# Two attentions of a decoder-like block joined into one pipeline of four phases, with the weights split a phase ahead

## The reference

```python
ln_out = ln(x)
q  = ln(fp8_linear(ln_out, wq,  ...))   # 16 heads, normalised per head
k  = ln(fp8_linear(ln_out, wk,  ...))   # 8 heads
v  =    fp8_linear(ln_out, wv,  ...)
core = gqa(q, k, v)                     # softmax(q k / sqrt(128)) v, per sequence
qx = ln(fp8_linear(ln_out, wqx, ...))
kx, vx = split(ctx @ w_kv_x.T);  kx = ln(kx)
xout = gqa(qx, kx, vx)
cat  = concat(core, xout)               # 32 heads of 128
x   += fp8_round(cat / smooth) @ wproj.T * (proj_in * proj_w)
```

## Time and profile before

| | us |
|---|---|
| runs (3): median, lowest, highest | 1149.35, 1148.18, 1149.48 |
| profiled execution | 1150.45 |
| its span in the profile | 1148.5 |
| TensorE busy in it | 890.5 (78%) |
| VectorE busy | 932.7 (81%) |
| ScalarE busy | 715.9 (62%) |
| GpSimd busy | 393.4 (34%) |

### The profile page before, as it was taken

The page is one execution under the profiler, slowest core; times in us unless marked ns, Lnnn a source line. Parts: engine busy times, 40 slices in busy tenths (PEclk is TensorE's granted clock), DMA queues, the critical chain, the costliest instruction groups (busy, mean ns, idle before and its releaser), DMA issues. The chain is left out here.

```text
span 1148.5 us, 23844 instructions
## 1 busy us (share of the span) xinstructions
PE 890.5 (78%) x6878; PEld 787.9 (69%) x6878; DVE 932.7 (81%) x2442; ACT 715.9 (62%) x2471; POOL 393.4 (34%) x498
## 2 busy tenths in 40 slices
PE   3720056621899999999999369999999999997738
PEld 3710033321788888888898358999999999996627
DVE  7989989878889889989988448888888888886460
ACT  3445034363888888888888457777777777774303
POOL 0008910000344444444444433333343333323024
PEclk9865589855999999999999679999999999998559
DMA  6021200001100000000000220000000000000400
GB/s 223 1 100 50 70 0 1 0 0 67 45 2 1 0 0 0 0 0 0 0 0 1 60 69 6 11 6 5 5 9 5 5 5 5 0 0 1 152 19 19
DMA packets 18266, 26.96 MB, mean 23 GB/s; under 512 B 1264, under 2 KB 15408, under 8 KB 17456
## 3 DMA queue, kind: packets, MB, share of 16 engines
q1 hardware_dynamic: 17840, 25.41, 6.5%
q0 software_dynamic: 384, 1.05, 0.3%
HBM read 23.83 MB, written 2.62 MB: 23 GB/s over the span
## 5 line engine op out<-in xcount | busy, mean ns | idle before, releaser
L1214 POOL TENSOR_TENSOR c_pn<-c_p,c_rsum 128x256 f32<-128x256 f32 x64 | 39.6, 619 | 216.4 <-DVE c_rsum L1337 216.4
L1251 DVE TENSOR_REDUCE c_v<-c_sq 128x6 f32<-128x768 f32 x64 | 60.7, 949 | 54.4 <-ACT c_sq L1394 54.2
L1214 POOL TENSOR_TENSOR s_pn<-s_p,s_rsum 128x256 f32<-128x256 f32 x64 | 39.6, 618 | 141.0 <-DVE s_rsum L1337 141.0
L1228 POOL TENSOR_TENSOR s_cat<-s_tb,s_mb 128x512 fp32r<-128x512 bf16 x64 | 73.9, 1154 | 34.6 <-DVE s_tb L1292 34.6
L1251 DVE TENSOR_REDUCE s_v<-s_sq 128x6 f32<-128x768 f32 x64 | 60.7, 949 | 28.5 <-ACT s_sq L1394 28.1
L1228 POOL TENSOR_TENSOR c_cat<-c_tb,c_mb 128x512 fp32r<-128x512 bf16 x64 | 74.0, 1156 | 28.8 <-DVE c_tb L1292 28.8
L1453 PE MATMUL s_pj_ps<-wp,s_cat 128*128 128x256 f32 x512 | 78.9, 298 | 1.6 <-POOL s_cat L1228 1.6
L1453 PE MATMUL c_pj_ps<-wp,c_cat 128*128 128x256 f32 x512 | 78.1, 296 | 1.8 <-POOL c_cat L1228 1.8
L1377 ACT ACTIVATE s_p<-s_kT_sc_ps,s_nmax 128x64 f32<-128x64 f32 x256 | 76.6, 311 | 2.8 <-DVE s_nmax L1258 2.4
L1377 ACT ACTIVATE c_p<-c_kT_sc_ps,c_nmax 128x64 f32<-128x64 f32 x256 | 76.6, 311 | 2.7 <-DVE c_nmax L1258 1.8
L1417 PE MATMUL c_qo_ps<-wq,c_xqf 128*128 128x512 f32 x256 | 75.9, 419 | 0.0
(11 more groups left out here) (359 smaller groups left out, 2912.8 us busy)
## 6 DMA issues: line engine op xcount, KB each, us to landing
x_res<-in_x SPq DMA_DIRECT2D x4, 512.0 KB, 6.0
vT<-in_ctxT SPq DMA_DIRECT2D x2, 1024.0 KB, 10.5
tf_work<-in_wqT SPq DMA_DIRECT2D x2, 1024.0 KB, 6.2
tf_work<-in_wprojT SPq DMA_DIRECT2D x2, 1024.0 KB, 5.5
w_work<-in_wqxT SPq DMA_DIRECT2D x2, 1024.0 KB, 6.6
w_work<-in_wkvxT SPq DMA_DIRECT2D x2, 1024.0 KB, 8.1
c_ctx<-in_ctxT SPq DMA_DIRECT2D x16, 128.0 KB, 2.2
w_work<-in_wprojT SPq DMA_DIRECT2D x2, 1024.0 KB, 7.9
```

The source lines that it names most:

```text
L1214: nc.gpsimd.tensor_tensor(pn[:].rearrange("p (a t) -> p a t", a=4), pe_s[:].rearrange("p (a t) -> p a t", a=4), rsum[:].unsqueeze(2).broad ...
L1228: nc.gpsimd.tensor_tensor(cat[out8.o % 2][:], tb[:], mb[:], ALU.subtract).then_inc(cat_ready, 1)
L1251: norm(nc.vector.tensor_reduce(v6[:], sq[:].rearrange("p (h d) -> p h d", d=D), AX.X, ALU.add))
```

## The change

- The two attentions are one stage and one pipeline of 128 units, with no loops: all steps are written out. It has four phases of 32 units. A phase takes half the heads of one kind over all 16 tiles: phases 0 and 1 are self, 2 and 3 cross. A unit is the same as before; a tile has two units in a phase.
- Weights are held in two sets of half the size. Phase i uses set i % 2. The weights of phase 0 are prepared in the ternary stage, as before, but they are half as many. Those of phase i + 1 are prepared in phase i, for all i below 3: heads (scale, sum, mean off) in steps 1 to 24, uppers of 128x256 on ScalarE in steps 5 to 28, lowers of 128x256 on GpSimd in steps 6 to 29 (those of v in phase 0, which need a scale, on VectorE).
- On GpSimd a step's order is: pn, head, lower part, cat, conversion.
- On TensorE the query transposes stand ahead of the value product.
- On VectorE the rounding instructions are interleaved with the Newton step, and the addition to x stands ahead of the normalised key; it adds two tiles at once (128x512), after each fourth unit. The projection now sums two units in PSUM.
- SyncE loads the q weights of phase 1 in the quant stage, the rest at the start of the attention, and those of later phases when GpSimd is done with the buffers.

The core of the diff:

```diff
+def first_weights_act(act, nc, aw, raw):
     act.wait_ge(aw["scales_ready"], 4)
+    for part, kind, n in (("q", 0, QC // D), ("k", 1, KVC // D)):
+        act.wait_ge(aw["arrived"][part], 16)
...
+def first_weights_pool(pool, nc, aw, raw, col):
...
+    pool.wait_ge(aw["scales_ready"], 4)
+    for h in range(KC):
+        half = raw["v"][:, h, :]
+        nc.gpsimd.tensor_scalar(half, half, scale_col(aw, 2, h), None, ALU.mult).then_inc(aw["sums_ready"], 1)
+    pool.wait_ge(aw["sums_ready"], KC)
+    split("v", 1)
+    pool.wait_ge(aw["arrived"]["p"], 16)
+    split("p", 2)
...
+        pool.wait_ge(aw["scaled"], nth + 1)
...
+        split(part, 3 + nth)
...
+FIRST_HEAD_AT, FIRST_UPPER_AT, FIRST_LOWER_AT = 1, 5, 6
...
+        def head_item(u):
+
+            i = u.o - FIRST_HEAD_AT
+            return Head(aw, raw_w, u.phase + 1, i) if u.phase + 1 < N_PHASES and 0 <= i < N_HEADS else None
...
             def _(pool):
...
+                convert(0)
+                for s in range(UNITS + 4):
+                    u, soft, out8 = At(s), At(s - 3), At(s - 4)
                     if soft.live:
...
                             rsum[:].unsqueeze(2).broadcast_to([P, 4, S]), ALU.mult).then_inc(pn_ready, 1)
+                    head = head_item(u) if u.live else None
+                    if head:
+                        pool.wait_ge(aw["head_scaled"], head.count)
+                        nc.gpsimd.tensor_tensor(head.sum, head.sum, minus_mean[:], ALU.mult).then_inc(aw["head_sum"], 1)
+                        pool.wait_ge(aw["head_sum"], head.count)
+                        nc.gpsimd.tensor_tensor(head.w, head.w, head.sum.broadcast_to([P, D]), ALU.add
+                                                ).then_inc(aw["head_centred"], 1)
+                    w, count = piece(u, FIRST_LOWER_AT) if u.live else (None, None)
+                    if w and w.scale is None:
+                        pool.wait_ge(aw["piece_upper"], count)
+                        pool.wait_ge(aw["piece_lower"], count - 1)
+                        nc.gpsimd.tensor_tensor(w.lower, w.raw, w.upper.bitcast(F32), ALU.subtract
+                                                ).then_inc(aw["piece_lower"], 1)
                     if out8.live:
+                        pool.wait_ge(cadd_ready, out8.count())
                         wait_unit(pool, pj_done, out8.before(2))
+                        nc.gpsimd.tensor_tensor(cat[out8.n % 2][:], tb[:], mb[:], ALU.subtract).then_inc(cat_ready, 1)
...
+                    if u.live and u.half == 0 and u.turn + 1 < N_PHASES * NT:
+                        wait_unit(pool, kv_done, u.before(1))
+                        wait_unit(pool, q_done, u.before(1))
+                        convert(u.turn + 1)
...
             def _(act):
...
+                        nc.scalar.activation(v_s[u.n % 4][:], kv_bank(u)[:, KW:2 * KW], ACT.Copy).then_inc(v_ready, 1)
+                        head = head_item(u)
+                        if head:
+                            if head.first:
+                                act.wait_ge(aw["arrived"][head.part], 16 * (u.phase + 2))
+                            nc.scalar.activation(head.w, head.w, ACT.Copy, scale=head.scale, accum_out=head.sum
+                                                 ).then_inc(aw["head_scaled"], 1)
+                        w, _ = piece(u, FIRST_UPPER_AT)
+                        if w:
...
+                            nc.scalar.activation(w.upper, w.raw, ACT.Copy, scale=1.0 if w.scale is None else w.scale
+                                                 ).then_inc(aw["piece_upper"], 1)
...
             def _(dve):
...
+                    if pj.live and pj.n % 4 == 3:
+
+                        dve.wait_ge(pj_done, pj.count())
+                        xt = x_res[:, pj.tile - 1:pj.tile + 1, :]
+                        nc.vector.scalar_tensor_tensor(xt, pj_ps[:], pscale[:], xt, ALU.mult, ALU.add
+                                                       ).then_inc(x_added, 1)
...
             def _(pe):
...
+                    if pj.live:
+                        wp = sets[pj.phase % 2]["p"]
+                        pe.wait_ge(cat_ready, pj.count())
...
+                        if u.o == 0 and u.phase:
+                            pe.wait_ge(aw["piece_lower"], N_PIECES * u.phase)
```

More of the change, by code:

```diff
@@ L599, in heads_of @@
[L599 to L621, removed]
@@ L624, in cross_chunks @@
[L624 to L639, removed]
@@ L642, in lower_part @@
[L642 to L653, removed]
-    act.wait_ge(aw["scales_ready"], 4)
[L656 to L660, removed]
+        lower=sem("w_lower"), head_scaled=sem("w_head_scaled"), head_sum=sem("w_head_sum"),
@@ new lines, with __init__ @@
+class Head:
+    def __init__(self, aw, raw, phase, i):
+        self.part, per = ("q", QC // D) if i < KC * QC // D else ("k", KVC // D)
+        h, a = divmod(i if self.part == "q" else i - KC * QC // D, per)
+        self.w = raw[self.part][:, h, a * D:(a + 1) * D]
+        self.sum = aw["sums"][:, i:i + 1]
+        self.first = h == 0 and a == 0
+        kind = {"q": 0, "k": 1}[self.part] if phase < 2 else {"q": 3, "k": None}[self.part]
+        self.scale = 1.0 if kind is None else scale_col(aw, kind, h)
+        self.count = N_HEADS * (phase - 1) + i + 1
@@ new lines, with __init__ @@
+N_PIECES = KC * (QC + 2 * KVC) // PIECE + PR
+class Piece:
+    def __init__(self, aw, raw, sets, phase, m):
+        self.first = False
+        for self.part, n in (("v", KC * KVC // PIECE), ("p", PR), ("q", KC * QC // PIECE), ("k", KC * KVC // PIECE)):
+            if m < n:
+                break
+            m -= n
+        self.first = m == 0
+        if self.part == "p":
+            at = (slice(None), m, slice(None))
+        else:
+            h, c = divmod(m, n // KC)
+            at = (slice(None), h, slice(c * PIECE, (c + 1) * PIECE))
+        self.raw = raw[self.part][at]
+        self.upper, self.lower = (t[at] for t in sets[phase % 2][self.part])
+        self.scale = scale_col(aw, 2, h) if self.part == "v" and phase < 2 else None
@@ L1067, in _, with __init__, count, before @@
                                                  scale=inv[:, a:a + 1]).then_inc(y_ready, 1)
[L1072 to L1085 removed]
+GU = 2
+HU = GU * HPG
+PER_PHASE = 2 * NT
+UNITS = N_PHASES * PER_PHASE
+class At:
+    def __init__(self, n):
+        self.n, self.live = n, 0 <= n < UNITS
+        self.phase, self.o = divmod(n, PER_PHASE)
+        self.cross = self.phase >= N_PHASES // 2
+        self.half = n % 2
+        self.turn = n // 2
+        self.tile = self.turn % NT
+        self.first_head = self.phase * PR + self.half * HU
+    def count(self, per=1, more=None):
+        return self.n * per + (per if more is None else more)
+    def before(self, units, per=1):
+        return None if self.n < units else (self.n - units + 1) * per
```

457 lines of the change are left out of this document (215 added, 242 removed).

## The result

| | before | after |
|---|---|---|
| median of 4 runs in one comparison, us | 1149.41 | 1259.23 |
| ratio, 95% interval | | 1.0951, 1.0929 to 1.0972 |
| span of the profiled execution, us | 1148.5 | 1257.2 |
| granted TensorE clock, mean | 0.883 | 0.88 |

The changed kernel takes 109.8 us more. The forecast was 1211, its range ended at 1250. The direction and the ring that causes it were right; a rival that I had kept apart, TensorE's clock, came true on top of it.

A forecast was written before the change was run, and what follows sets the result against it. TensorE was taken as full in both attentions, with ring steps bound by GpSimd's cat after the change. Profiled 1150.45 - 28 - 42.4 + 131.9 + 0.5 gave 1212.5, so a forecast median of 1211 us, range 1180 to 1250.

The forecast's parts named there:

- the ring: Attention steps with heads: cat queued behind GpSimd's wait for ScalarE's head delays projection; 7.44 or 6.76 us a step, +131.9.
- TensorE's clock: Rival, 12%: in ring steps TensorE's idle 2 us lower its clock; 1246 or 1280 us.
- The ternary stage: Before the attentions: half the weights to prepare, so GpSimd holds VectorE for less time; gain 28 us.
- the bound I had named: Ternary stage: gain only 22 us if the sixteen normalisations before 85.71 are held as well.
- The junction: Between self- and cross-attention: one pipeline turns the 47.96 us into one step of 5.6; gain 42.4 us.
- the contention that I had priced at 0 to 0.2: Ring steps: VectorE's fast forms lengthen GpSimd's chain, 0 to 0.2 us a step, 0 to 14 in all; taken as 0.
- the rival's case of a quarter of the steps: Clock at 1.2 GHz in a quarter of the 69 ring steps, some 2 us each: +35, 1246 us.
- The orders on TensorE and VectorE: Attention steps: query transposes ahead of value product, rounding interleaved with Newton; remove waits of 0.1 us, counted as nothing.
- A: Rival, 10%: in the attention steps the wait for the head is covered, TensorE stays full, gains remain; 1080 us.
- C: Rival, 12%: VectorE and GpSimd hold each other far more in ring steps, 8.0 us a step, +38; 1249 us.
- the end: Very end of the kernel: the projection's sum, added every fourth step, adds 0.5 us.

The follow-up runs named there:

- the late split: Changed kernel with GpSimd's cat and conversion ahead of the head, plus GpSimd starting the first weights' split only at the first quantised tile: 1081.91 us.
- its gap filled: Changed kernel plus 14 spare identity transposes on TensorE before the projection in each step that follows a head: 1222.95 us, ratio 1.0636.
- cat first: Changed kernel with GpSimd's order made softmax scaling, cat, conversion, head, lower part: 1092.14 us, ratio 0.9501.
- value product first: Changed kernel with GpSimd's cat and conversion ahead of the head, plus TensorE's value product ahead of the query transposes again: 1082.41 us.
- both kernels that open the ring: Changed kernel with GpSimd's cat and conversion ahead of the head (1092.14 us), or with ScalarE's head at the front of its step (1088.27 us).

## Why the prediction was right in its mechanism and wrong in its size

- *The ternary stage: gain 28, measured 22.4.* GpSimd's work was costed at 30 us and took 81.23 to 116.51, 35.3. I had taken its durations from the rows where they were short. Here the sums' scaling took 0.89, the centring of 1024 columns 2.5 and a copy of 2048 2.43, each beside VectorE's held forms; in the late split, where VectorE is in the tile pipeline, they have 0.52, 2.0 and 1.91. That VectorE ends when GpSimd does was right (reduction at 116.89), and 22 was the bound I had named for normalisations that are held as well. They were: fifteen of them took 10.63, and VectorE's ternary work began at 90.56 in place of 85.71.
- *The junction: 42.4, measured 42.1.* Right.
- *The ring: 7.44 and 6.76 a step, measured 7.36 to 7.60 and 6.77.* Right in each of its parts: 1.60, then 1.30 to the cat with a lower part and 0.62 without, 1.20, 3.35. In 34 steps the cat took 1.28 in place of 1.15 beside VectorE's rounding, and its result came as much later, the contention that I had priced at 0 to 0.2. These steps lie 0.15 above my 7.44, and most of the others with a lower part 0.08 below it. Against the forecast's 131.9 stand 133.6 in the trace (173.4 by which the 126 steps grew, less 39.8 for the clock), and 130.8 between the changed kernel with its gap filled, 1222.95, and the one with cat first, 1092.14.
- *The clock: this is the step that failed.* The forecast took the ring's products at 2.4 GHz throughout and put the clock at nothing, as a rival of 12%. In fact 26 of 69 steps had their products in part at 1.2 GHz, 1.53 us each, 39.8; filling the gap gave back 36.3. Both rows that I had on it I read wrongly. The 0.64 of the drain came, I wrote, "after gaps like these"; the longest gap in front of it is 0.81 us and not 2, so the row spoke more for the rival than I made of it. Against it I put "184 to 188 shows 1.00 at a busy share of 2.57 in 4, less than the ring's 5.37 in 7.44". That is one window of a stage in which the clock can go either way: the kernel before keeps 1.00 there from 153.7 to 215, with TensorE busy 65% of the time, and the changed kernel loses it at 179.8 at the same 65%, with no pause over 1.17 us since 150.

The kernel before, its clock in the ternary stage and in the drain, and the longest pause ahead of the latter:

```profile
153.70:215.00 61.30, 40.12 (x297) 23.99 (x298) 57.26 (x167) 28.70 (x68) 0.00 (x0) 1.00 0.00 0
631.50:634.80 3.30, 3.30 (x18) 3.28 (x16) 2.04 (x6) 1.94 (x10) 1.34 (x2) 0.50 0.00 0
```

```profile
629.65 0.44 PE L1499 MATMUL s_qo_ps<-ident,s_pn 128*128 128x128 f32 x2 [0.81 <-POOL s_pn L1214]
```

The changed kernel, in the ternary stage:

```profile
150.00:179.80 29.80, 19.29 (x142) 11.61 (x143) 27.48 (x79) 13.34 (x33) 0.00 (x0) 1.00 0.00 1
179.90:186.60 6.70, 6.00 (x27) 3.05 (x26) 6.37 (x21) 2.79 (x6) 0.00 (x0) 0.50 0.00 0
```

So neither a stage's busy share nor the length of one pause tells by itself whether the clock falls. What the runs give is how often it did: after 24 of 53 pauses of 1.80 to 2.13 us, after 2 of 16 of 1.32 in the same kernel and 4 of 69 with the lower part behind the cat, and after none of at most 0.45 with the gap filled. The price of such a step was set at some 2 us and found at 1.53, and the rival's case of a quarter of the steps gave 35: near the 39.8, but by luck, with too few steps at too high a price. It belonged in the forecast. TensorE: Matmul & The Clock Gate, Part 1, of the Trainium skill says that activity releases a clock which is low by default. The filled gap agrees with it: more work, less time.

- *The orders on TensorE and VectorE at nothing:* near the truth in sum, by two errors against each other. With cat first, where TensorE is full, the 126 steps take 2.9 us more than in the kernel before. TensorE's order alone costs 7.2 (value product first takes them back), so the rest of the change gives some 4 back; which part of it does was not tried.
- *The rivals A and C.* A (the wait covered) did not come, but both kernels that open the ring land near where it pointed: 1080, plus 5.6 for the ternary stage and 2.9 for the steps, makes 1088.5; measured 1092.1 and 1088.3. C (8.0 a step by contention) had a fifth of its size.

The forecast's profiled execution was 62.0 above the one before; the two spans differ by 108.7. By stage the difference is whole: the steps 173.4 in place of 131.9 (41.5 more, of which 39.8 are the clock), the first query 22.7 earlier in place of 28 (5.3 more), the junction 42.1 in place of 42.4 (0.3 more), the end 0.1 in place of 0.5 (0.4 less). The medians differ by 1.1 us more than the spans, which is within the runs' scatter. Why the lower clock takes some steps and not the like ones beside them is open, and the order of VectorE's rounding was not tried by itself.

## What to carry to other kernels

Before moving work within an engine's queue, ask which of the following items needs less than the moved one waits for: here a head that waits for ScalarE's last result but one of the same step stood ahead of a cat that the next projection needs, and cost 131 us; either of two moves, on GpSimd or on ScalarE, gave it all back. When a new wait lets TensorE pause on every step, count the lower clock as a term of the sum: the same busy share of 65% went with either clock here, and shortening the pause from some 2 us to 1.3 brought the long steps from 26 to 4 of 69. And take the duration of GpSimd's and VectorE's instructions from rows where both engines are as busy as they will be.

## What the runs showed of the hardware that I had not expected

- After a recurring pause of 1.80 to 2.13 us in a self-attention step of 7.4 to 7.6 (7.8 to 8.1 in the cross-attention) TensorE's granted clock fell in 24 of 53 steps (0.95 and 0.97 as means over 100 us); after one of 1.32 it fell in 2 of 16, and in 4 of 69 of the kernel that has the lower part behind the cat. It also fell in the drain of the kernel before, where no pause in front of it was over 0.81. Fourteen transposes that nobody reads made the kernel 36.3 us faster.
- GpSimd's own instructions grow by contention too: a scaling of 128x16 from 0.30 to 0.89, a copy of 128x2048 from 1.91 to 2.43, each with a held VectorE instruction beside it.
- With TensorE full, the place of four transposes and eight small products relative to each other is worth 0.06 us of 5.4, although neither waits for anything. Where in TensorE that time goes the traces don't show.
